# Second attention of a two-layer post-norm transformer: each head in its own 32-row band, heads multiplied in pairs

## The reference

```python
c_k = x @ w_dk + b_dk;  c_v = x @ w_dv + b_dv          # 128 -> 128
k = c_k @ w_uk + b_uk;  v = c_v @ w_uv + b_uv
q = split_heads(x)                                     # 16 heads of 8 features; k, v the same way
q = _apply_rope(q, cos, sin);  k = _apply_rope(k, cos, sin)
attn = softmax(einsum('bhid,bhjd->bhij', q, k) * scale)  # 256 x 256 a head, no mask
out = einsum('bhij,bhjd->bhid', attn, v) ... @ w_o + b_o
```

## Time and profile before

| | |
|---|---|
| median of 3 runs | 1376.44 us |
| the profiled execution | 1379.24 us, span 1377.5 us, mean granted TensorE clock 0.974 |
| busy over the span | PE 1264.0 (92%), PEld 1076.6, DVE 970.8 (70%), ACT 921.5 (67%), POOL 620.4 (45%) |
| second attention | from 772 us (its first matmul) to the last exponential at 1158.2 us |

### The profile page before, as it was taken

The page is one execution under the profiler, slowest core; times in us unless marked ns, Lnnn a source line. Parts: engine busy times, 40 slices in busy tenths (PEclk is TensorE's granted clock), DMA queues, the critical chain, the costliest instruction groups (busy, mean ns, idle before and its releaser), DMA issues. The chain is left out here.

```text
span 1377.5 us, 34255 instructions
## 1 busy us (share of the span) xinstructions
PE 1264.0 (92%) x10765; PEld 1076.6 (78%) x10765; DVE 970.8 (70%) x2980; ACT 921.5 (67%) x2433; POOL 620.4 (45%) x965
## 2 busy tenths in 40 slices
PE   5999999999999998899999699999989987878876
PEld 5888888888888887899999577777677765567765
DVE  6787777777777777676678578888878873633333
ACT  4777777677777666456676578777777766656643
POOL 3244444444444443544544435555555523445552
PEclk9999999999999999999999899999999999988997
DMA  8021202020202021132113321220242002032216
GB/s 269 21 76 43 90 27 90 27 90 27 90 27 90 27 87 57 38 95 67 57 55 130 117 62 34 87 82 22 83 149 71 15 11 93 16 94 82 80 45 189
DMA packets 56597, 100.24 MB, mean 73 GB/s; under 512 B 11200, under 2 KB 46400, under 8 KB 53888
## 3 DMA queue, kind: packets, MB, share of 16 engines
q1 hardware_dynamic: 46848, 79.41, 18.3%
q0 software_dynamic: 9088, 18.89, 3.9%
q10 hardware_dynamic: 576, 0.86, 0.2%
HBM read 78.16 MB, written 62.06 MB: 102 GB/s over the span
## 5 line engine op out<-in xcount | busy, mean ns | idle before, releaser
L632 ACT ACTIVATE a_prob<-psum,a_nmx 128x128 f32<-128x128 f32 (+1 forms) x512 | 208.3, 425 | 72.5 <-DVE a_nmx L998 72.5
L868 POOL TENSOR_TENSOR a_prob<-a_prob,a_rl 128x128 f32<-128x128 f32 (+1 forms) x256 | 124.3, 507 | 241.4 <-DVE a_rl L1002 240.7
L366 DVE TENSOR_REDUCE f_nmx<-psum 128x2 f32<-128x512 f32 x256 | 170.9, 686 | 34.1 <-PE psum L210 30.2
L639 ACT ACTIVATE a_probt<-psum 128x768 f32<-128x768 f32 x128 | 104.8, 819 | 80.3 <-PE psum L1434 80.3
L2439 ACT ACTIVATE a_prob<-psum 128x1024 f32<-128x1024 f32 x128 | 127.4, 1024 | 24.1 <-PE psum L2154 14.3
L915 POOL DMA_INDIRECT yt<-a_yrow,a_dest x78 | 78.9, 1011 | 99.8 <-ACT a_yrow L681 82.7
L1790 POOL DMA_INDIRECT yt<-m_yrow,m_dest x78 | 76.6, 982 | 70.0 <-DVE m_yrow L1937 49.2
L632 ACT ACTIVATION_READ_ACCUMULATOR a_prob<-psum,a_nmx 128x1 f32 x512 | 107.9, 211 | 0.0
L987 DVE TENSOR_TENSOR a_qkt<-psum,a_bqk 128x512 f32<-128x512 f32 x128 | 88.2, 689 | 27.0 <-PE psum L109 24.3
L1434 PE MATMUL psum<-ident,a_prob 128*128 128x128 f32 x768 | 105.3, 273 | 1.1 <-DVE a_prob L1008 0.7
L107 PE MATMUL psum<-a_x_h,a_wqk_h 128*128 128x256 f32 x312 | 93.7, 300 | 3.9 <-issue 2.0
(11 more groups left out here) (412 smaller groups left out, 3910.2 us busy)
## 6 DMA issues: line engine op xcount, KB each, us to landing
xs<-in_fill SPq DMA_DIRECT2D x144, 264.0 KB, 4.2
a_xrow<-xs SPq DMA_DIRECT2D x39, 132.0 KB
m_xrow<-xs SPq DMA_DIRECT2D x39, 132.0 KB
f_yin<-yt SPq DMA_DIRECT2D x18, 256.0 KB, 2.8
w<-in_w SPq DMA_DIRECT2D x16, 256.0 KB, 3.4
f_yin<-yt SPq DMA_DIRECT2D x7, 512.0 KB, 8.4
f_w<-in_wr SPq DMA_DIRECT2D x2, 1284.0 KB
xs<-in_fill_idle SPq DMA_DIRECT2D x2, 1056.0 KB, 6.3
```

Of the source, the lines that this page charges most:

```text
L366: nc.vector.reduce_max(f.nmx[:, :, h:h + 1], bank.rearrange("p (q k) -> p q k", q=QB), AX.X, negate=True).then_inc(f.mx_done, 1)
L632: last = nc.scalar.activation(prob[:, hp % 4, h, at], S[:, 2 * (hp % 2) + h, at], ACT.Exp, bias=nmx[:, hp % 4, q, h:h + 1], accum_out=lsum ...
L639: nc.scalar.activation(probt[:, hp % 2], PT[:, :, 0:SW], ACT.Copy).then_inc(pt_done, 1)
L868: last = nc.gpsimd.tensor_tensor(prob[:, hp % 4, 0, at], prob[:, hp % 4, 0, at], rl[:, hp % 4, 0, q:q + 1].to_broadcast(prob[:, hp % 4, 0, ...
```

## The change

Each head gets a band of 32 rows of its own, four bands a group: 24 rows for the three products, and 8 free rows that take the maxima (in q) and the markers (in k). q and k of a group stand side by side in one tile, `stk[p][:, group, 0 or 1, :]`, so k is not masked and both are copied out of PSUM at once. Heads 2i and 2i+1 lie in two different bands, and their matmuls are issued alternately, into two different banks. The two banks R0 and R1 are now one pair R, filled by four matmuls (`pair`) and reduced by one DVE instruction. The markers come from one more matmul a group. The maxima are turned at the start of the next pass and DVE adds them to q's rows. Two groups' stacks are made together and copied by one ACT instruction, 128x1024, and the rounding of q and k to their high parts moves from DVE to ACT (`high`).

Cut to its core:

```diff
 def stack(k, bank):
     for j in range(2):
-        out = bank[0:KR, j * T:(j + 1) * T]
+        out = bank[:, j * T:(j + 1) * T]
         nc.tensor.matmul(out, f.sel[:, 2 * j, k, :], f.qk_h[:, j, :], start=True, stop=False)
-        last = nc.tensor.matmul(out, f.sel[:, 2 * j + 1, k, :], f.qk_l[:, j, :], start=False, stop=True)
-    last.then_inc(f.stack_ps, 1)
+        last = nc.tensor.matmul(out, f.sel[:, 2 * j + 1, k, :], f.qk_l[:, j, :], start=False, stop=j == 0)
+    return nc.tensor.matmul(out, f.marker[:, k, :], f.one_row, start=False, stop=True)

-def first_scores(h, p, bank):
-    for q in range(QB):
-        last = nc.tensor.matmul(bank[:, q * T:(q + 1) * T], f.q_stk[p][0:KR, h // HG, q * P:(q + 1) * P],
-                                f.k_stk[p][0:KR, h, :], start=True, stop=True)
+def first_scores(h, q, p, bank):
+    rows = slice(LOW * (h % HG), LOW * (h % HG + 1))
+    return nc.tensor.matmul(bank[:, q * T:(q + 1) * T], f.stk[p][rows, h // HG, 0, q * P:(q + 1) * P],
+                            f.stk[p][rows, h // HG, 1, :], start=True, stop=True)

+def pair(i, p):                                            # PE
+    for q in range(QB):
+        for c in range(2):
+            last = first_scores(2 * i + c, q, p, R[:, c, :])
+    last.then_inc(pair_ps, 1)

 def scores(t, p):                                          # PE
-    for h in (2 * t, 2 * t + 1):
-        out = ST[:, 2 * (t % 2) + h % 2, :]
-        for k in range(QB):
-            ... k_stk[p][:, h, k * P:(k + 1) * P], q_stk[p][:, h // HG, :] ...
+    for k in range(QB):
+        for h in (2 * t, 2 * t + 1):
+            rows = slice(LOW * (h % HG), LOW * (h % HG + 1))
+            ... stk[p][rows, h // HG, 1, k * P:(k + 1) * P], stk[p][rows, h // HG, 0, :] ...

+def maxima(i, count):                                      # DVE, 8 a batch; before 16 of one bank
+    dve.wait_ge(pair_ps, count)
+    nc.vector.reduce_max(f.nmx[:, :, 2 * i:2 * i + 2].rearrange("p q h -> p h q"), R.rearrange(...), AX.X, negate=True
+                         ).then_inc(pair_done, 1)

+def add_maxima(p, bank, n):                                # DVE, first of a pass
+    dve.wait_ge(f.mt_ps, n)
+    nc.vector.tensor_tensor(q_rows, q_rows.bitcast(F32), bank[:, 0:T]...to_broadcast([P, NGR, T]), ALU.add
+                            ).then_inc(f.mt_done, 1)

+def two_stacks(k, p, banks, count):                        # ACT, twice a batch; five instructions a group before
+    act.wait_ge(both_ps, count)
+    nc.scalar.activation(stk[p][:, k:k + 2]..., banks, ACT.Copy).then_inc(both_act, 1)
+def high(j, total, ready, signal, n):                      # ACT, twice a batch; on DVE before
...
+    def first(i):                                          # PE, in place of first(0) to first(15)
+        if i == 0: pe.wait_ge(both_act, n * 2 + 2)
+        elif i == NPR // 2 and turned: pe.wait_ge(both_act, n * 2 + 3)
+        else: pe.wait_ge(pair_done, n * NPR + i)
+        pair(i, 1 - p)
```

## The result

Four runs of the changed kernel gave a median of 1434.83 us (1433.81 to 1435.52), against 1375.87 us before on the same chip: a ratio of 1.0436, 95% interval 1.041 to 1.0461. That is 59 us slower. The forecast was 1387, within 1362 to 1403; it had the sign and missed the size more than fivefold.

The account below looks back on a forecast made before the run. The prediction took the PE-DVE chain to bound the loop, and PE the experts of layer 0. Its terms, -7 + 8.8 + 5.5 + 3 = +10.3 us on the median of 1376.44, gave 1387, range 1362 to 1403.

Parts of the forecast that it names:

- The ring, 24.1 a pass: Second attention's loop: PE and DVE alternate on one pair of banks; eight maxima once round sum to 24.1 us, 24.2 before.
- The step of 5.5: Loop, end of the eighth maximum to next batch's first: stacks, turned maxima, addition, scores, tail's heads and division, 5.5 us.
- Late signals, +.9 a pass: Loop, while POOL scatters: PE's signals come late and are no longer hidden, .9 us a pass; with it the loop +8.8.
- Start, -7: Batches 0 and 1: fewer copies, no markers and shorter first passes bring batch 2 to 826.5 instead of 833.43, -7 us.
- Experts of layer 0, +5.5: Experts' stage, PE full: 16 groups of 32-row matmuls each pay mode switches and exposed weights, .35 a group, +5.5 us.
- End, +3: Last batches: the ring has no less in it, 24.4; +1.2 for batch 13, +2.8 for batch 14, a little back, +3.
- Bands side by side: Pairs and scores on PE: matmuls in two bands run together, so 32 take the steps of 16.
- The first, that late signals miss the ring (1376): Rival, 20%: PE's late signals don't delay the loop, which stays at 24.1 us a batch; 1376 us.
- The two that were slower: Rivals: late signals on two or three hand-overs, 1400 us (14%); bands' weights not loading side by side, 1403 us (6%).
- The faster one, that the ring doesn't bind: Rival, 17%: scores and exponentials drive a pass, so less work means less time, 22.7 us a batch; 1356 us.

Follow-up runs that it names:

- the kernel with all rows: The changed kernel with first scores and scores taking all 128 rows, same order and banks, against the kernel before: ratio 1.0257 to 1321.07 us.
- the reordered kernel with all rows: The changed kernel with all 128 rows in both products, first pair ahead of scores and tail's heads, second one place earlier: 1389.06 us, ratio 1.0074 to the kernel before.
- the later set: The changed kernel again, on one chip with the kernel before (1377.9 us) and two reordered versions: 1443.97 us, ratio 1.0482.
- the reordered kernels: The changed kernel with its first two pairs moved earlier, against the kernel before: ratio 1.0399 in bands of 32 rows, 1.0074 with all 128 rows.

## Why the prediction was wrong

The step that failed is the one under all the others: durations of PE were taken from rows at full clock, 2.4 GHz, and used for a kernel whose pairs and scores take 32 rows and run side by side. Its granted clock in the loop is .79 to .84. "No engine is full, so what counts is the chain between them" left the clock out; no rival had it either, though the kernel before has it at .83 in its own batch 0. The range would have held the time without that: 1434.8 less the 36 us worked out below is 1399, within 1362 to 1403 by a narrow margin.

- *The ring, 24.1 a pass.* Right: 24.4 at full clock, each of its eight steps within .2. It gives 12 x (24.4 - 24.2), +2.4 us. The step of 5.5, from one batch's last maximum to the next one's first, measured 5.66, and its parts come out one by one: the turned maxima start 1.33 behind the last maximum (forecast 1.39), the tail's heads end at 4.81 (4.65). The remaining 36 us of the loop's 38.7 come with the lower clock, 3.0 a pass: shown by the one pass without a fall beside those with one, and by the kernel with all rows, which has none.
- *Late signals, +.9 a pass.* Wrong: it measured under .1. In the quick pass the tail's heads were turned by 870.69 and DVE began at 870.74, with a scatter running. In every pass of this trace that hand-over takes .04. Of the loop's 96 pairs one reaches DVE late, by .94 (at 1062.38), which is .08 a pass. The turned heads reach ACT late by .34 to 1.73 in six passes, and PE never waits for them. The rows of the quick pass:

```profile
869.60 1.09 PE L2170 MATMUL psum<-ident,a_osb 128*128 128x128 f32 x8
```

```profile
870.74 0.37 DVE L2677 RECIPROCAL a_rs<-psum 128x16 f32<-128x16 f32 x2 [0.95 <-PE psum L2170]
```

```profile
870.16 0.96 POOL L2577 DMA_INDIRECT xs<-a_nrm,a_idx  x1 [0.30 <-issue]
```

So a scatter that is running doesn't by itself make PE's signal late, here on a chip of the slower kind. The trace of the kernel before says so too, at the start of its batch 13, with scatters issued as ever:

```profile
1098.55 1.09 PE L2174 MATMUL psum<-ident,a_osb 128*128 128x128 f32 x8
```

```profile
1098.63 0.96 POOL L2591 DMA_INDIRECT xs<-a_nrm,a_idx  x1 [0.30 <-issue]
```

```profile
1099.68 0.37 DVE L2687 RECIPROCAL a_rs<-psum 128x16 f32<-128x16 f32 x2 [1.08 <-issue]
```

That is 1099.68 - 1099.64 = .04. On the quicker chip the kernel before, with its markers apart, hands over in .04 in every pass, also with a scatter running across it (884.56 to 885.71, the hand-over at 885.68), and there its passes are 23.2 without the alternation of 23.6 and 24.8. The reordered kernel with all rows, on a slower chip, has DVE late by .23 to .38 in the loop. What makes signals late on the one kind of chip is open; nothing was tried on it.

- *Start, -7.* Measured +2.8. The first exponential comes 10.8 us behind the first stack, not 11.7 as before, so the copies saved .9 and not 2.4; and batches 0 and 1 took 26.5 and 26.4 at a clock of .68 and .81, where 22.0 and 22.7 were forecast. The clock is only part of this miss: in the kernel with all rows batch 1 has full clock and takes 26.8, more than the 25.7 of its loop. So the ring isn't shorter in the first passes, as the term had it; what lengthens it there is open.
- *Experts of layer 0, +5.5.* Right in sign and too large. The stack at 778.09 comes 5.6 later than before, but batch 0's first stack, where the changed work on PE begins, already comes 1.7 later (700.37 against 698.63); in the later set it comes 1.3 earlier. Between the two stacks the time is 77.7 against 73.8, and in the later set 77.6 against 73.9: +3.9 and +3.7, inside the bounds 0 to 6. With all rows it is 73.1, and 73.0 in the reordered kernel. So short rows and their switches cost some 4.6 in this stage, and the rest of the change saves .8. The rule that a change of tiling mode drains PE (the Trainium skill, TensorEngine Tiling (Array Packing), Key Properties) agrees with that.
- *End, +3.* Measured +8.2 up to the last exponential: 25.4 and 17.4 us for batches 14 and 15, where the term, less its 1.2 for batch 13, had some +1.8. Most of the miss is the clock again: it was .68 and .50 in these batches, and the kernel with all rows, at full clock, takes 24.5 and 12.9, which is +2.8.
- *Bands side by side.* Right, and more than forecast: where scores and a pair lie in four different bands, all four run together, as these rows of the quick pass show, 885.56 being the next start:

```profile
885.10 0.38 PE L2150 MATMUL psum<-a_stk 32*128 32x256 f32 x2
885.12 0.38 PE L214 MATMUL psum<-f_stk 32*128 32x256 f32 x2
```

- *The rivals.* None had the time. The first, that late signals miss the ring (1376), was right in what it said of the ring: 24.4 at full clock, with next to nothing for them. The two that were slower reached 1400 and 1403 by other mechanisms, which the ring's steps exclude. The faster one, that the ring doesn't bind, is excluded by the quick pass and by the reordered kernels.

## What to carry to other kernels

Don't price a matmul by a full-clock row of the kernel before without asking what clock the changed kernel will be granted: where a change lowers the rows of many of PE's matmuls and lets them run side by side, look first at the row of the granted clock in each stage, and reckon the stage once more with doubled steps. An engine that gets 2 us of work less a pass gains nothing when a single buffer makes a ring of it and its reader; draw the ring once round and put the waits of others outside it. And a stretch at half clock in the kernel before is a place to look for a gain: parting one 3.6 us instruction of another engine and moving it into idle time gave .4%.

## What the runs showed of the hardware

The granted clock can fall though PE is busy nearly all the time by its records: PE busy 239 of 250 us and the clock .73 with 32 rows in both products, against 240 and .98 with 64 rows, 247 and 1.00 with 32 rows in the first scores alone, and 219 and 1.00 with all rows in the changed kernel. Whether it's the rows or the running side by side that counts isn't parted by these runs. Added matmuls of 32 rows raise it in part (.79 to .87 in the loop). The Trainium skill (TensorE: Matmul & The Clock Gate, What's actually happening) has the clock go by how busy PE is and names idle time as what lets it fall. In batch 0 of the kernel before the trace agrees: the clock falls to half within a wait of 3.27 us. In the loop with 32 rows PE was busier by the records than in the kernel before (239 against 233 of 250 us), and its clock fell, so the records' busy time alone doesn't tell it.

Chips differ: the kernel before took 1376 to 1379 us on some and 1320 to 1322 on others, and the ratio of the changed one was 1.044 to 1.048 on the former and 1.053 on the latter.
